# Two edits to a decoder kernel: softplus on VectorE alone with delta first, and normalisation with means and variances in turn

## The chip, the cores and the metric

The kernel runs on one core of a Trainium2 chip. Its time is device microseconds from the start to the end of one execution, and the median of several executions counts. TensorE (PE) multiplies matrices into PSUM, VectorE (DVE), ScalarE (ACT) and GpSimd (POOL) work on tiles in SBUF or PSUM, SyncE (SP) issues most DMAs. Each engine has its own in-order program, and semaphores order them against each other. All data is float32 unless said otherwise.

## The reference

A decoder of six blocks over x of shape (2, 1024, 256): a Mamba block, cross attention, a causal attention with a mixture of experts, linear attention, a second cross attention and a feed-forward net. Each block gets `_layernorm(x)` and adds its result to x. Two parts matter here.

```python
def _layernorm(x, axis=-1, eps=1e-05):
    m = jnp.mean(x, axis=axis, keepdims=True)
    v = jnp.var(x, axis=axis, keepdims=True)
    return (x - m) / jnp.sqrt(v + eps)
...
xn = _rmsnorm(x, norm_w)
...
dA = jnp.exp(d_t[..., None] * A)
dBu = (d_t * u_t)[..., None] * B_t[:, None, :]
h = dA * h + dBu
y = jnp.einsum('bdn,bn->bd', h, C_t)
```

In the Mamba block, `xn` is projected to `xm` and `z`; `xm` goes through a causal convolution of four taps and a silu and becomes u; u is projected to a low-rank part, B and C; the low-rank part is projected to delta, and delta = softplus(delta + bias). The scan over time then runs 64 states for each of 512 channels.

## The kernel before, in words

X lies channels first, 128 partitions by 2 x 2048 columns, and is worked in four chunks (`NCH`) of 512 columns (`W`).

**`norm`** (lines 91 to 215) is called nine times: for the Mamba block (start 12.71 us), its rms norm without centring and with weights (46.83), cross attention (1583.92), the decoder's outer norm (1753.25), its first norm with weights and biases (1778.86), the experts' norm with weights and biases (2341.35), linear attention (2683.59), the second cross attention (2804.14) and the feed-forward net (2880.66). TensorE forms the mean of each chunk over channels by a product with a matrix of 1/256 (L132); VectorE subtracts it (L146); ScalarE squares (L178); TensorE forms the variance the same way (L138); ScalarE takes an approximate reciprocal root (L181) and its square (L184); VectorE makes one Newton step of three operations (L152, L155, L157). Chunks 0 and 1 are scaled by GpSimd (L199), chunks 2 and 3 by VectorE (L160); with weights, ScalarE applies them last (L172). Each step runs over all four chunks before the next one begins on the same engine. The block ends with a barrier of all engines, which also waits for the weights that SyncE loads beside it.

**`scan_inputs`** (lines 420 to 719) runs once for each of two batches, starting at 67.94 and 825.90 us. TensorE makes 38 tiles in the order of a list (`order`, L446), each into one of eight PSUM banks in turn; tile n waits until tile n - 8 was taken from its bank. The 1024 columns of a batch are two halves. ScalarE takes most tiles (L551), applies silu to u (L576) and makes |delta| (L582), its exponential e (L584), max(delta, 0) (L585) and four squares of e shifted by constants (L595). log(1 + e) is then a polynomial: products of (square + constant), formed one behind the other. VectorE computes it for three of the four channel groups (`softplus_dve`, operations of 1536 columns), GpSimd for the fourth (`softplus_pool`, 12 operations of 512 columns a half). The results are delta and delta times u, which TensorE transposes (tiles `du`) and ScalarE (half 0) or VectorE (half 1) copies out. ScalarE also forms the scan's first products (L607). SyncE stores u, C and delta to DRAM and reads delta of half 0 back, spread over partitions (`near`). There is room for three squares (`ROOM`), so a fourth waits until the first was used up, by both engines.

**`scan`** follows each `scan_inputs`, with 512 scans on VectorE (L876), decays and products on ScalarE (L839, L847), weighting on GpSimd (L825) and transposes and sums on TensorE; its code is the same before and after.

## Time and profile before

| | us |
|---|---|
| median of 3 runs | 3047.18 |
| lowest, highest | 3044.08, 3047.55 |
| the profiled execution's own time | 3044.58 |
| span of its trace, first to last instruction | 3042.8 |
| mean granted TensorE clock | 0.913 of full speed |
| busy: PE, DVE | 2370.3, 1997.0 |
| busy: ACT, POOL | 1772.5, 1398.9 |

The trace is of one execution. Busy times are sums over one engine; the time between an instruction's start and the end of the idle time before it is put down to what released it. A program of this kind is a row of stages with barriers between them, so the lengths of the stages add up to the whole, and shares of busy time over the whole span say little of one stage.

### The profile page before, as it was taken

The page shows a single profiled execution, that of the slowest core. Times are in us where ns is not written, and L with a number is a line of the kernel's source. Part 1 is how long each engine was busy: PE and PEld are TensorE (multiplying, and loading weights), DVE is VectorE, ACT ScalarE, POOL GpSimd, SP SyncE. Part 2 cuts the span into 40 slices and gives each one's busy share as a digit, 9 for nine tenths or more (in the row PEclk, how much of TensorE's full clock was granted, in tenths as well). Part 3 has the DMA queues.
Part 4 walks back from the last instruction along what each step waited for, and adds up shares of the span by engine and source line. Part 5 has one row for each costly group of instructions (what it writes and reads, how often), then busy time and mean ns, then how long its engine had stood idle before and what let it go on. Part 6 is the DMA issues. An engine that isn't in the chain of part 4 may idle for free. (4 is left out here: it accounts for less than half of the span.)

```text
span 3042.8 us, 38732 instructions
## 1 busy us (share of the span) xinstructions
PE 2370.3 (78%) x12420; PEld 1202.1 (40%) x12421; DVE 1997.0 (66%) x1798; ACT 1772.5 (58%) x2733; POOL 1398.9 (46%) x540
## 2 busy tenths in 40 slices
PE   4678888888857888888886758797787499869668
PEld 1244444444324444444435123223222355545323
DVE  5689999999658999999965666515913222133440
ACT  3689999999478999999941430171064111122230
POOL 1489998999557999899941110000000300020000
PEclk7889999999988999999996878798889699979889
DMA  2130001000123000100000300010012300010000
GB/s 75 54 106 28 24 28 39 28 28 28 40 72 87 28 28 28 39 28 24 28 20 2 112 35 1 6 42 11 1 33 100 157 21 21 23 39 9 28 0 28
DMA packets 59819, 116.17 MB, mean 38 GB/s; under 512 B 13620, under 2 KB 21812, under 8 KB 58305
## 3 DMA queue, kind: packets, MB, share of 16 engines
q1 hardware_dynamic: 51104, 103.72, 10.6%
q0 software_dynamic: 8608, 11.05, 1.2%
q8 instruction: 65, 1.06, 0.1%
q14 instruction: 42, 0.34, 0.0%
HBM read 86.92 MB, written 27.53 MB: 38 GB/s over the span
## 5 line engine op out<-in xcount | busy, mean ns | idle before, releaser
L825 POOL TENSOR_TENSOR hs<-hs,c_bc 128x2048 f32<-128x2048 f32 x256 | 1166.2, 4556 | 67.0 <-DVE hs L876 49.3
L876 DVE TENSOR_TENSOR_SCAN hs<-decays,carry,ps 128x512 f32<-128x512 f32 x512 | 621.7, 1270 | 9.1 <-PE ps L903 8.4
L876 DVE TENSOR_TENSOR_SCAN hs<-decays,ps 128x512 f32<-128x512 f32 x512 | 610.9, 1215 | 21.0 <-PE ps L903 8.3
L911 PE MATMUL ps<-hs,sel 128*64 128x512 f32 x2048 | 498.4, 608 | 15.5 <-POOL hs L825 15.2
L839 ACT ACTIVATE decays<-delta_near,A 128x512 f32<-128x512 f32 x512 | 363.4, 723 | 23.2 <-DVEq L853 22.7
L903 PE MATMUL ps<-ident,dbu_even 128*128 128x128 f32 x2048 | 295.1, 283 | 91.9 <-DVE hs L876 63.2
L903 PE MATMUL ps<-ident,dbu_odd 128*128 128x128 f32 x2048 | 293.3, 282 | 92.3 <-DVE hs L876 60.6
L839 ACT ACTIVATE decays<-delta_far,A 128x512 f32<-128x512 f32 x512 | 358.8, 714 | 11.0 <-DVE hs L876 10.9
L847 ACT ACTIVATE dbu_odd<-du_turned,b_turned 128x512 f32<-128x512 f32 x512 | 360.8, 718 | 0.0
L847 ACT ACTIVATE dbu_even<-du_turned,b_turned 128x512 f32<-128x512 f32 x496 | 349.8, 718 | 0.0
L903 PEld LDWEIGHTS ps<-ident,dbu_even 128*128 128x128 f32 x2048 | 220.0, 141 | 241.9 <-DVE hs L876 192.5
L903 PEld LDWEIGHTS ps<-ident,dbu_odd 128*128 128x128 f32 x2048 | 219.6, 141 | 242.2 <-DVE hs L876 188.4
L1058 ACT ACTIVATE prob<-ps 128x1024 f32<-128x1024 f32 (+2 forms) x224 | 176.1, 837 | 161.7 <-PE ps L1029 137.5
L911 PEld LDWEIGHTS ps<-hs,sel 128*64 128x64 f32 x2048 | 124.5, 136 | 213.1 <-issue 188.0
L981 POOL DMA_DIRECT2D q<-o_rows x13 | 9.1, 698 | 399.1 <-DMA o_rows<-osb 334.4
L1183 PE MATMUL ps<-kx,qx 32*128 32x77 f32 (+4 forms) x1280 | 138.5, 553 | 53.4 <-DVE negmax L1210 30.1
L1067 DVE COPY osb<-ps 128x512 f32<-128x512 f32 x32 | 21.8, 689 | 215.5 <-PE ps L1040 215.5
L1210 DVE TENSOR_REDUCE negmax<-ps 128x4 f32<-128x2048 f32 (+4 forms) x70 | 139.0, 2029 | 23.3 <-PE ps L1188 16.6
L1614 PE MATMUL ps<-w_wv,x_turned 128*128 x304 | 141.1, 608 | 10.7 <-ACT x_turned L1673 10.7
L1709 DVE TENSOR_SCALAR hid_turned<-ps 128x512 f32<-128x512 f32 x38 | 26.3, 691 | 178.6 <-PE ps L1622 178.6
L1023 PE MATMUL ps<-qx,kx 32*128 32x512 f32 (+4 forms) x896 | 112.7, 574 | 38.7 <-PEq L1231 20.4
L199 POOL TENSOR_TENSOR XN<-XN,norm_rstd 128x1024 f32<-128x1024 f32 x8 | 18.8, 2344 | 246.5 <-DVE norm_rstd L157 246.5
(265 smaller groups left out, 2759.1 us busy)
## 6 DMA issues: line engine op xcount, KB each, us to landing
c_bc<-c_rows SPq DMA_DIRECT2D x256, 128.0 KB, 2.8
o_rows<-osb SPq DMA_DIRECT2D x32, 256.0 KB
u_rows<-u SPq DMA_DIRECT2D x4, 1024.0 KB, 8.8
d_rows<-delta SPq DMA_DIRECT2D x4, 1024.0 KB, 4.2
delta_near<-d_rows SPq DMA_DIRECT2D x4, 1024.0 KB, 9.6
hs<-u_rows SPq DMA_DIRECT2D x4, 1024.0 KB, 6.6
delta_far<-d_rows SPq DMA_DIRECT2D x4, 1024.0 KB, 12.1
w_down<-in_expert_proj SPq DMA_DIRECT2D x1, 4096.0 KB, 36.5
```

What stands on the lines that cost most here:

```text
L825: pool.tensor_tensor(x, x, spread(c_bc[:, g, :], 4), ALU.mult).then_inc(weighed.sem, 1)
L839: act.activation(decays[:, s % RING, :], (far if q else near)[:, blk, :], ACT.Exp, scale=A[:, at(i * GB, g), blk]).then_inc(decay.sem, 1)
L847: act.activation(dbu[0], dbu[1], ACT.Copy, scale=dbu[2]).then_inc(made.sem, 1)
L876: dve.tensor_tensor_scan(hs[:, quad % RING, n, :], decays[:, s % RING, :], ps[:, DBU + s % RING, :], carry[:, at(i * GB, g), blk] if q els ...
L903: mm = pe.transpose(ps[:, DBU + s % RING, t * P:(t + 1) * P], room[g % 2][:, t, blk, :, :].rearrange("p n d -> p (n d)"), k.ident[:])
L911: mm = pe.matmul(ps[lo:lo + DB, ACC + quad % 2 * 2 + j // 2, :], k.sel2[:, :], hs[:, quad % RING, j, :], start=False, stop=False, skip_gro ...
L1023: mm = pe.matmul(ps[0:krows, 2 * (m % 3) + j % 2, first:W], job.kx[rows, par, c, t * P:t * P + krows], job.qx[rows, par, c, qc * W + first ...
L1058: act.activation(prob[0:krows, m % 4, :, first:W], ps[0:krows, 2 * (m % 3):2 * (m % 3) + 2, first:W], ACT.Exp).then_inc(weighed.sem, 1)
L1183: mm = pe.matmul(ps[:, STRIPS * (f % 2) + j, at:at + m], qx[strip, par, c, t * P:(t + 1) * P], kx[strip, par, c, o:o + m], start=True, sto ...
L1210: dve.tensor_reduce(to[:, :, groups[0]:groups[0] + per], banks[:, :, :, 0:m], AX.X, ALU.max, negate=True).then_inc(maxed.sem, 1)
L1614: mm = pe.matmul(ps[:, 2 * h + g, :], xt[:, p, c, :], wv[:, bass.ds(e * (C * 2 * FF) + (c * 2 * FF + g * FF + h * HALF), HALF)], start=(c ...
L1709: dve.tensor_scalar(hid_t[:, h, :, :], ps[:, HID + h, :].rearrange("p (f n) -> p f n", f=HT), 1.0, None, ALU.mult).then_inc(hid_copied.sem, 1)
```

## The change

**In `norm`**, TensorE forms mean 0, mean 1, then a variance and a mean in turn. ScalarE squares chunk c and then takes the root of chunk c - 1, and begins with a root of one column that has no use but that it is the first of its kind. The Newton step is written with a third, small operation on ScalarE (the root times -0.5) and two on VectorE instead of three: (v r r - 3)(-r / 2). VectorE centres chunk c ahead of inverting chunk c - 2.

```diff
+            def means(c):
...
+            for c in range(NCH + 1):
+                if centre and c < NCH:
+                    means(c)
+                if c:
+                    variances(c - 1)
+
...
-                dve.tensor_scalar(rstd[:, c, :], rstd[:, c, :], -0.5, 1.5, ALU.mult, ALU.add).then_inc(corrected.sem, 1)
-                dve.wait_ge(corrected.sem, corrected.at(c + 1))
-                dve.tensor_tensor(rstd[:, c, :], rstd[:, c, :], r0[:, c, :], ALU.mult).then_inc(rstd_ready.sem, 1)
-                if c >= BY_POOL:
-                    dve.wait_ge(rstd_ready.sem, rstd_ready.at(c + 1))
-                    dve.tensor_tensor(chunk(dst, c), chunk(body, c), spread(rstd[:, c, :], C),
-                                      ALU.mult).then_inc(scaled_dve.sem, 1)
+                dve.wait_ge(halved.sem, halved.at(c + 1))
+                dve.scalar_tensor_tensor(rstd[:, c, :], rstd[:, c, :], 3.0, r0[:, c, :], ALU.subtract, ALU.mult)\
+                   .then_inc(rstd_ready.sem, 1)
...
+            for c in range(NCH + 2):
+                if centre and c < NCH:
+                    centre_chunk(c)
+                if c >= 2:
+                    invert(c - 2)
+                    if c - 2 >= BY_POOL:
+                        scale(c - 2)
...
+            def root(c):
+                act.wait_ge(var_ready.sem, var_ready.at(c + 1))
+                act.activation(r0[:, c, :], ps[:, VAR + c, :], ACT.Abs_reciprocal_sqrt,
+                               bias=k.eps[:, 0:1] if eps == EPS else k.eps[:, 1:2]).then_inc(root_ready.sem, 1)
+                act.wait_ge(root_ready.sem, root_ready.at(c + 2))
+                act.activation(r0sq[:, c, :], r0[:, c, :], ACT.Square).then_inc(root_squared.sem, 1)
+                act.wait_ge(root_squared.sem, root_squared.at(c + 1))
+                act.activation(r0[:, c, :], r0[:, c, :], ACT.Copy, scale=-0.5).then_inc(halved.sem, 1)
+
...
+            act.activation(first[:], k.eps[:, 0:1], ACT.Abs_reciprocal_sqrt).then_inc(root_ready.sem, 1)
+            for c in range(NCH + 1):
+                if c < NCH:
+                    square(c)
+                if c:
+                    root(c - 1)
```

**In `scan_inputs`**, all of the polynomial is VectorE's, in operations of 2048 columns. The list of tiles has delta right behind the low-rank part, and `z` of half 1 last. ScalarE takes |x| and max(x, 0) straight from the PSUM bank, by Abs and Relu with the bias, and e lies in the room of `du_turned` instead of `xm`. SyncE stores u of both halves first.

```diff
-    e_ = xm[:, :, :].rearrange("p c n -> p (c n)")[:, 0:CPB * CI * W].rearrange("p (h c n) -> p h c n", h=CPB, c=CI)
+    e_ = du_t[:, :, :].rearrange("p (h c) n -> p h c n", h=CPB)
...
-                                                 ("C", 0, 1), ("delta", 0, CI), ("B", 0, 1), ("z", 1, CI),
-                                                 ("low", 1, 1), ("C", 1, 1), ("delta", 1, CI), ("B", 1, 1),
-                                                 ("du", 0, QT), ("du", 1, QT)) for m in range(tiles)]
+                                                 ("delta", 0, CI), ("C", 0, 1), ("low", 1, 1),
+                                                 ("delta", 1, CI), ("C", 1, 1), ("B", 0, 1), ("B", 1, 1),
+                                                 ("z", 1, CI), ("du", 0, QT), ("du", 1, QT)) for m in range(tiles)]
...
-            def take_delta(h):
+            def magnitude_of(h):
                 for m in range(CI):
-                    take("delta", h, m, delta[:, m, h * W:(h + 1) * W], ACT.Identity, bias=vec[:, m, DC + 1:DC + 2])
+                    act.wait_ge(summed.sem, summed.at(index["delta", h, m] + 1))
+                    act.activation(e_[:, h, m, :], bank(("delta", h, m)), ACT.Abs, bias=vec[:, m, DC + 1:DC + 2])\
+                       .then_inc(magnitude.sem, 1)
+
+            def positive_of(h):
+                for m in range(CI):
+                    take("delta", h, m, delta[:, m, h * W:(h + 1) * W], ACT.Relu, bias=vec[:, m, DC + 1:DC + 2])
...
             silu_u(0)
             take_z(0)
             take_low(0)
-            take_delta(0)
+            magnitude_of(0)
+            silu_u(1)
+            exponential(0)
+            squares(0, range(ROOM))
+            positive_of(0)
+            take_low(1)
+            magnitude_of(1)
+            squares(0, range(ROOM, PAIRS))
+            exponential(1)
+            positive_of(1)
             take_b(0)
-            silu_u(1)
+            take_b(1)
+            squares(1, range(PAIRS))
             take_z(1)
-            exponential(0)
-            squares(0)
-            take_low(1)
-            take_delta(1)
-            take_b(1)
-            exponential(1)
-            squares(1)
             first_products()
...
-            for h in range(CPB):
-                softplus_pool(pool, h)
...
+
+            store_u(0)
+            sp.wait_ge(u_stored.sem, u_stored.at(16))
+            store_u(1)
+            store_c(0)
+            sp.wait_ge(c_stored.sem, c_stored.at(16))
+            store_delta(0)
+            sp.wait_ge(d_stored.sem, d_stored.at(16))
+            spread_delta(k, sp, b, 0, near, d_near)
+            store_c(1)
+            store_delta(1)
```

`softplus` is `softplus_dve` with `part` and `DVE_PART` gone, and without the wait for `positive`; `softplus_pool` is gone.

What stands on ScalarE in the normalisation at 1583.92, before and then now (`norm_r` is the root, `norm_r0sq` its square):

```order
L178 ACTIVATE norm_sq<-XN 128x1024 x4
L181 ACT_TABLE_LOAD
L181 ACTIVATE norm_r_67<-ps,eps 128x512
L184 ACTIVATE norm_r0sq<-norm_r_67 128x512
L181 ACTIVATE norm_r_67<-ps,eps 128x512
L184 ACTIVATE norm_r0sq<-norm_r_67 128x512
```

```order
L205 ACT_TABLE_LOAD
L205 ACTIVATE norm_first<-eps 128x1
L184 ACTIVATE norm_sq<-XN 128x1024 x2
L188 ACTIVATE norm_r_69<-ps,eps 128x512
L191 ACTIVATE norm_r0sq<-norm_r_69 128x512
L193 ACTIVATE norm_r_69<-norm_r_69 128x512
L184 ACTIVATE norm_sq<-XN 128x1024
L188 ACTIVATE norm_r_69<-ps,eps 128x512
```

The table load stands at the front, and the first root comes behind two squares instead of four.

On VectorE in a norm (the first call, whose chunks lie in `dbu_even`), before and then now:

```order
L146 TENSOR_TENSOR dbu_even<-X,ps 128x2x512 x4
L152 SCALAR_TENSOR_TENSOR norm_rstd<-ps,norm_r0sq 128x512
L155 TENSOR_SCALAR norm_rstd<-norm_rstd 128x512
L157 TENSOR_TENSOR norm_rstd<-norm_rstd,norm_r_21 128x512
L152 SCALAR_TENSOR_TENSOR norm_rstd<-ps,norm_r0sq 128x512
```

```order
L152 TENSOR_TENSOR dbu_even<-X,ps 128x2x512 x3
L159 SCALAR_TENSOR_TENSOR norm_rstd<-ps,norm_r0sq 128x512
L163 SCALAR_TENSOR_TENSOR norm_rstd<-norm_rstd,norm_r_21 128x512
L152 TENSOR_TENSOR dbu_even<-X,ps 128x2x512
L159 SCALAR_TENSOR_TENSOR norm_rstd<-ps,norm_r0sq 128x512
```

The fourth centring stands behind the inversion of chunk 0.

On ScalarE in `scan_inputs` of the first batch, from the take of half 0's low-rank part (`low`) on, before and then now. `xm` and, now, `du_turned` hold e:

```order
L551 ACTIVATE low<-ps 128x512
L551 ACTIVATE delta<-ps,mamba_vec 128x512 x4
L551 ACTIVATE b_turned<-ps 128x256
L576 ACTIVATE u<-u,mamba_vec 128x512 x4
L551 ACTIVATE zs<-ps 128x512 x4
L582 ACTIVATE xm<-delta 128x2048
L584 ACT_TABLE_LOAD
L584 ACTIVATE xm<-xm 128x2048
L585 ACTIVATE delta<-delta 128x4x512
L595 ACTIVATE sp_square<-xm,roots 128x2048 x4
L551 ACTIVATE low<-ps 128x512
```

```order
L572 ACTIVATE du_turned<-ps,mamba_vec 128x512 x4
L583 ACTIVATE u<-u,mamba_vec 128x512 x4
L588 ACT_TABLE_LOAD
L588 ACTIVATE du_turned<-du_turned 128x2048
L597 ACTIVATE sp_square<-du_turned,roots 128x2048 x3
L552 ACTIVATE delta<-ps,mamba_vec 128x512 x4
L552 ACTIVATE low<-ps 128x512
L572 ACTIVATE du_turned<-ps,mamba_vec 128x512 x4
L597 ACTIVATE sp_square<-du_turned,roots 128x2048
L588 ACTIVATE du_turned<-du_turned 128x2048
```

`z` of half 1 (`zs`) no longer stands ahead of the exponential, the fourth square stands behind the Abs of half 1, and later in the same program `zs` has a table load of its own, as has the first decay of `scan`.

## Rows read from the trace of the kernel before

**Rows 1.** Busy time by stretch: bounds, length, busy us (instructions) per engine, clock, DMA.
```profile
12.71:40.40 27.69, 16.38 (x32) 6.91 (x32) 17.59 (x18) 11.69 (x14) 4.69 (x2) 0.83 0.24 86
46.83:67.63 20.80, 8.99 (x16) 3.70 (x16) 12.71 (x14) 14.38 (x20) 4.69 (x2) 0.75 0.00 0
1583.92:1609.18 25.26, 13.97 (x32) 5.96 (x32) 17.58 (x18) 10.45 (x13) 4.68 (x2) 0.85 0.15 48
...
1778.86:1805.95 27.09, 15.66 (x32) 6.61 (x32) 17.60 (x18) 15.24 (x20) 4.69 (x2) 0.81 0.25 97
2341.35:2368.18 26.83, 13.97 (x32) 5.96 (x32) 17.59 (x18) 16.52 (x21) 4.68 (x2) 0.83 0.95 370
2683.59:2710.46 26.87, 15.56 (x32) 6.61 (x32) 17.60 (x18) 10.45 (x13) 4.69 (x2) 0.82 0.13 42
2804.14:2828.00 23.86, 13.97 (x32) 5.97 (x32) 17.59 (x18) 9.27 (x12) 4.69 (x2) 0.90 0.11 28
...
67.94:166.50 98.56, 61.45 (x152) 29.01 (x152) 56.97 (x53) 58.65 (x66) 46.94 (x29) 0.78 0.26 77
825.90:922.55 96.65, 58.37 (x152) 27.93 (x152) 55.89 (x53) 56.99 (x64) 43.96 (x24) 0.81 0.23 68
166.80:806.00 639.20, 537.67 (x3088) 285.18 (x3088) 618.53 (x516) 623.41 (x1016) 594.07 (x192) 0.99 0.12 38
```

**Rows 2.** Timeline of the normalisation at 1583.92: start, us, engine, line, operation [idle before].
```profile
1585.91 1.22 DVE L146 TENSOR_TENSOR XN<-X,ps 128x1024 f32<-128x1024 f32 x1 [2.31 <-PE ps L132]
...
1587.16 1.06 ACT L178 ACTIVATE norm_sq<-XN 128x1024 f32<-128x1024 f32 x1 [34.65 <-DVE XN L146]
...
1593.39 1.28 ACT L181 ACT_TABLE_LOAD   x1
...
1594.68 0.69 ACT L181 ACTIVATE norm_r<-ps,eps 128x512 f32<-128x512 f32 x1
...
1595.40 0.63 ACT L184 ACTIVATE norm_r0sq<-norm_r 128x512 f32<-128x512 f32 x1
...
1596.14 0.69 DVE L152 SCALAR_TENSOR_TENSOR norm_rstd<-ps,norm_r0sq 128x512 f32<-128x512 f32 x1 [3.86 <-ACT norm_r0sq L184]
...
1598.10 2.35 POOL L199 TENSOR_TENSOR XN<-XN,norm_rstd 128x1024 f32<-128x1024 f32 x1 [37.08 <-DVE norm_rstd L157]
...
1598.65 2.07 DVE L155 TENSOR_SCALAR norm_rstd<-norm_rstd 128x512 f32<-128x512 f32 x1
```

**Rows 3.** Timeline of the first batch's scan inputs, by engine.
```profile
94.36 0.60 ACT L551 ACTIVATE low<-ps 128x512 f32<-128x512 f32 x1 [2.83 <-PE ps L542]
...
102.42 2.55 ACT L576 ACTIVATE u<-u,mamba_vec 128x512 f32<-128x512 f32 x4
...
116.19 5.77 ACT L595 ACTIVATE sp_square<-xm,roots 128x2048 f32<-128x2048 f32 x3
...
97.83 3.70 PE L526 MATMUL ps<-low,dbu_odd 128*128 128x512 f32 x8
...
125.90 5.81 PE L526 MATMUL ps<-low,dbu_odd 128*128 128x512 f32 x8 [10.05 <-ACT low L551]
...
118.21 1.76 DVE L473 SCALAR_TENSOR_TENSOR sp_poly<-sp_square,xm 128x1536 f32<-128x1536 f32 x1 [19.59 <-ACT sp_square L595]
120.11 4.68 DVE L473 SCALAR_TENSOR_TENSOR sp_poly<-sp_square,sp_poly 128x1536 f32<-128x1536 f32 x2
...
127.09 2.70 DVE L475 SCALAR_TENSOR_TENSOR sp_poly<-xm,sp_poly 128x1536 f32<-128x1536 f32 x1
...
168.50 2.33 DVE L876 TENSOR_TENSOR_SCAN hs<-decays,ps 128x512 f32<-128x512 f32 x2 [2.00 <-PE ps L903]
...
120.53 2.64 POOL L501 TENSOR_TENSOR sp_poly<-sp_poly,sp_square 128x512 f32<-128x512 f32 x1
...
160.72 1.26 POOL L505 TENSOR_TENSOR u<-delta,u 128x512 f32<-128x512 f32 x1
```

**Rows 4.** Groups of VectorE by shape: count | busy us, mean ns | idle before.
```profile
L1930 DVE TENSOR_TENSOR tern_room<-tern_room,w 128x2048 f32<-128x2048 f32 x2 | 4.6, 2292 | 0.1
```

More of the change, by code:

```diff
@@ L207, in norm @@
         centred.passed(NCH)
[L208 removed]
+    for s in (squared, var_ready, root_squared, newton, halved, rstd_ready):
         s.passed(NCH)
+    root_ready.passed(NCH + 1)
     scaled.passed(BY_POOL)
@@ new lines, in softplus @@
+                dve.wait_ge(soft.sem, soft.at(n + f))
+            dve.scalar_tensor_tensor(poly[:], square[:, (h * PAIRS + f) % ROOM], b, poly[:] if f else e,
+                                     ALU.add, ALU.mult).then_inc(soft.sem, 1)
+        dve.wait_ge(soft.sem, soft.at(n + PAIRS))
+        dve.scalar_tensor_tensor(poly[:], e, LOG1P_REAL, poly[:], ALU.add, ALU.mult).then_inc(soft.sem, 1)
+        dve.wait_ge(soft.sem, soft.at(n + PAIRS + 1))
+        dve.wait_ge(taken.sem, taken.at(take_no["delta", h, CI - 1]))
@@ L578, in exponential, with squares @@
             def exponential(h):
-                x = delta[:, :, h * W:(h + 1) * W]
-                act.wait_ge(taken.sem, taken.at(take_no["delta", h, CI - 1]))
-                act.activation(e_[:, h], x, ACT.Abs).then_inc(magnitude.sem, 1)
-                act.wait_ge(magnitude.sem, magnitude.at(h + 1))
+                act.wait_ge(magnitude.sem, magnitude.at((h + 1) * CI))
                 act.activation(e_[:, h], e_[:, h], ACT.Exp, scale=-1.0).then_inc(e_ready.sem, 1)
-                act.activation(x, x, ACT.Relu).then_inc(positive.sem, 1)
                 act.wait_ge(e_ready.sem, e_ready.at(h + 1))
-            def squares(h):
-                for f in range(PAIRS):
+            def squares(h, which):
+                for f in which:
                     n = h * PAIRS + f
@@ L678, in _, with store_u @@
             d_rows = k.d_rows[b].rearrange("(c p) t -> p c t", p=P)
-            for h in range(CPB):
+            def store_u(h):
                 cols = slice(h * W, (h + 1) * W)
```

121 lines of the change are left out of this document (41 added, 80 removed).

## The prediction

> **What bounds the kernel now.** I read first how long each stage lasts, then the timeline inside one normalisation, then the timeline of the scan inputs. [rows 1] gives a length per stage. The column after the bounds is the length, then come the busy times. The nine calls of `norm` last 20.8 to 27.7 us each, and in none is an engine busy for the whole length: VectorE has 12.7 to 17.6, TensorE 9.0 to 16.4, ScalarE 9.3 to 16.5, GpSimd 4.7. A stage in which nobody is full is bound by a chain. `scan_inputs` lasts 98.56 and 96.65 us for the two batches, with VectorE at 57, ScalarE at 59 and GpSimd at 47: a chain again. `scan` (639.2 us a batch) has ScalarE at 623 and VectorE at 619, and its code is not changed.
>
> [rows 2] is the normalisation that starts at 1583.92. VectorE centres a chunk 1.99 us after the start (four matmul passes of 0.43 us and 0.28 us until VectorE moves). ScalarE squares it (1.06), but the first root comes only at 1594.68: all means stand ahead of the variances on TensorE, all squares ahead of the roots on ScalarE, and a table load of 1.28 us lies between. Then each chunk takes root 0.69, square 0.63, three operations on VectorE. While GpSimd scales a chunk (2.35 us), the multiply-add of L155 lasts 2.07 us instead of 0.43, the time in which GpSimd works. Operations with one input in PSUM (L152, 0.69) are not held up.
>
> [rows 3] is the first batch. `low` of half 0 is taken at 94.36, but ScalarE reaches the exponential only after `z` of half 1, and VectorE stands idle 19.59 us before its first product at 118.21. Two neighbouring products of 1536 columns take 4.68 us, one alone 1.76, while a GpSimd product that starts at 120.53 takes 2.64: the two engines hold each other up. The last product is GpSimd's at 160.72; the stage ends at 166.50.
>
> **The change, part by part.**
>
> *Normalisation, centred, without weights.* I chain the new order with the same durations, from 0: mean 0 to 1.71; centred 1.99 to 3.21; squared 3.24 to 4.30; variance 0 from 4.35 to 6.06 (TensorE waits 0.9 us behind mean 1, all that the new wait costs); then mean 2 to 7.78, variance 1 to 9.49, mean 3 to 11.21. VectorE centres chunk 3 from 11.49 to 12.71. Queued behind it are the two operations on chunk 1 (0.69 each), which end at 14.03. GpSimd scales chunk 1 until 16.40. The second operation on chunk 2 has both inputs in SBUF and is late next: it ends 0.55 after GpSimd, at 16.95. Then scale 2 (1.22), two operations (0.69 each) and scale 3 (1.22), with 0.03 us between dependent ones and 0.08 us of overlap between others, give 20.78. The same chain for the old order gives 24.95, and the trace has 25.26, so the new one should last 21.1: **4.2 us less**. The early activation costs nothing, its load lies in the 1.99 us in which ScalarE has nothing to square. The extra ScalarE operation (0.63) ends at 12.25 for chunk 1 and delays nobody.
>
> This holds for four calls (1583.92 and two like it, at 1753.25 and 2880.66, and 2683.59, where the slow clock adds the same to both orders): 16.8 us. The first call (27.69) has the clock down for some 5 us, through all means; in the new order only the first means meet it before the chain turns to other engines: 5.0. The one at 2804.14 had no load inside (23.86): 2.8. Of the two with weights and biases, ScalarE becomes the end: its last halving comes at 17.8, then eight operations of 0.76 us ((16.52 - 10.45) / 8), 23.9 against 26.83: 2.9 at 2341.35, and 2.0 at 1778.86, which had no load to lose. The uncentred one (20.80) gains 0.7: its squares now queue behind roots. Sum **30.2 us** over nine calls.
>
> *Scan inputs.* Up to the take of `low` at 94.36 to 94.96 nothing moves. `delta` (0.86 us a tile, from 3.70 for four with the drain) now starts at once instead of behind C, at 95.0. The four Abs straight from PSUM end at 99.4, silu of half 1 (2.55) at 101.9, table load 103.2, Exp (taken as a square of the same form, 1.93) 105.1, three squares 110.8. The four Relu (0.61 each) and `low` of half 1 end at 113.7. `delta` of half 1 then finds the clock down, as at 125.90 (5.81 us where 3.70 is the full-speed price), since TensorE has idled 8 us: the Abs end at 119.6, the fourth square of half 0 at 121.6. That is the new wait: VectorE has finished its third product at 113.9 and stands still for 7.8 us. From there VectorE is never idle: four operations of half 0 to 131.0, C 0.6, seven of half 1 to 147.9, and the last transposes and copies (now from 160.72 + 1.26 to 166.50: 4.5) 152.4, against 166.50: **14.1 us less a batch**. The operations of 2048 columns are new; none in this stage shows them. L1930 takes 2.29 with both inputs in SBUF [rows 4], four thirds of 1.76 are 2.35, and four thirds of the longest, 2.70 at 127.09 [rows 3], are 3.6. I take 2.30, the nearest row in form, since with GpSimd gone nothing is left to contend. Both batches: 28.2 us.
>
> The removed GpSimd work (24 operations) was on the path and takes nothing with it. Stores: u of half 1 now leaves at 102, so its multiply does not wait; delta of half 1 leaves at 145.6 and has 7 us to land before the stage ends.
>
> *Table loads.* Silu of `z` 1 now comes after the exponentials, so each batch gets one more load there, in ScalarE's slack (it would be idle 7 us at the end), and one more at the first decay of `scan`. VectorE's first scan waits 2.00 us for TensorE at 168.50 [rows 3]; a decay 1.28 us later is 0.4 us too late at least, 1.28 at most because ScalarE is 97% busy there. I take 0.9 each, **1.8 us back**. The trace has 1.28 us for a load and the next activation starts 0.01 us after it (1593.39, 1594.68). The Trainium skill (ScalarE: Activation LUTs, What ACT_TABLE_LOAD costs) adds about 1.38 us of draining, 2.66 us in all; by that the scan starts would cost up to 2.8 us more, and the forecast 2993. The trace does not agree: nothing of that kind lies between the last square and the root.
>
> **Sum.** 30.2 + 28.2 - 1.8 = 56.6 us off the profiled execution's 3044.58: 2988.0. The median of the runs is 2.6 us above that execution, so I forecast **2990**.
>
> **The rivals.**
> *The clock (slower than before).* Now TensorE runs means and variances in one unbroken stretch; the new order has breaks of 0.9 us between chunks. If the granted clock fell to 1.2 GHz for them, four passes would take 3.41 instead of 1.71 us, and the same chain ends at 31.6 without weights and 35.3 with them, that is 3.9 to 7.7 us worse than now for the six and 8.2 and 8.5 for the two, 52 us in all, against 27 won elsewhere: 3044.6 + 25 + 2.6 = 3072. It decides where a centred call gets more than 3.4 us (27 / 8) longer than now. Against it: in `scan` TensorE is busy 538 of 639 us with many short breaks and keeps 0.99 [rows 1]; the new norm has it busy 14.0 of 15.6 us. The Trainium skill (TensorE: Matmul & The Clock Gate, Part 1) speaks for the danger in kind: idleness throttles the array again. 3%.
> *The wide operations are slow by themselves.* If 2.70 us were the price of such an operation and not contention, 2048 columns would take 3.6, fourteen of them 50 us after 107, and the stage would end where it does now: 3044.6 - 30.2 + 1.8 + 2.6 = 3019. For: 4.68 for two. Against: 1.76 for the same operation when GpSimd does not read. 5%.
> *Norms give half.* If ScalarE's three operations a chunk or GpSimd's hold of VectorE cost more than I chain, or the affine tail grows: 15 us less, 3005. 10%.
> *More comes.* After each norm TensorE idles some 12 us now, with the clock down at the next stage; idling 5.6 us less, it may keep it, up to 2.0 us (8.99 for the sixteen passes of the call at 46.83, 13.97 / 2 at full speed) at five places: 2980. 12%.
> *It doesn't do what it says*: the order of instructions shows the new order on each engine, so only a wait can undo it. Under 1%.
>
> **How the numbers follow.** The forecast itself has 69%. Its own bounds are 2.29 to 2.35 us for the wide operations (2 us over both batches), 0.8 to 2.6 for the scan starts, and 1 us per norm: 2980 to 3002. The range 2976 to 3008 adds the cases of half-norms and more clock, and leaves out the other two and their neighbourhood. About 0.2% (6 us) is what a measurement can tell from no change. Faster 0.95; within 0.2% 0.02; slower 0.03, the clock.
>
> **What would show it.** Right: norms without weights last 21.1 us, with GpSimd's second scaling starting 14 us in; the wide operations last 2.3 us each; VectorE idles about 8 us after three of them in half 0 and hardly after; `scan_inputs` lasts 84.5 us; nine norms lose 30 us together. Wrong: a granted clock under 0.8 while a norm's matmuls run, wide operations over 2.6 us, DMA or ScalarE ahead of the last copy of the stage, or a `scan` longer by more than 3 us.

## The result, and the profile after

The changed kernel takes **2993.19 us** (median of 4 runs, 2991.77 to 2994.59), against 3045.63 for the kernel before (4 runs, 3042.93 to 3047.55): ratio 0.9831, 95% interval [0.9816, 0.9847]. The span of the profiled execution is 2990.6 us, 52.2 shorter than that of before.

| | before | after |
|---|---|---|
| nine calls of `norm`, sum of their lengths, us | 229.3 | 197.6 |
| scan inputs, batch 0 and 1, us | 98.56, 96.65 | 85.17, 83.07 |
| from the start of `scan` to the next stage, batch 0 and 1, us | 659.1, 661.1 | 664.8, 660.4 |
| span, us | 3042.8 | 2990.6 |

A norm's length runs from its first matmul to its last operation (the uncentred one from its first operation of ScalarE, the decoder's outer norm up to the start of the norm behind it); that of the scan inputs from the first matmul to VectorE's last copy. The norms give 31.7 us, the inputs 27.0, and `scan` with the projection behind it takes 5.0 back. That makes 53.7; the span fell by 52.2, so the rest of the program took 1.5 more.

By stage, as [rows 1] shows it of before (stretch, its length, then busy time and instructions of PE, PEld, DVE, ACT and POOL, the granted clock, DMA share, GB/s; the stretch of the second batch's scan inputs, 812.05 to 895.39, runs on to the start of `scan`, 0.27 us behind the last copy):

```profile
12.62:35.31 22.69, 16.74 (x32) 6.65 (x32) 13.04 (x14) 13.16 (x18) 4.71 (x2) 0.98 0.29 105
41.85:61.85 20.00, 10.09 (x16) 3.76 (x17) 8.34 (x10) 16.38 (x26) 4.72 (x2) 0.76 0.00 0
61.85:147.02 85.17, 60.21 (x152) 27.34 (x152) 57.42 (x53) 57.13 (x71) 3.17 (x5) 0.82 0.29 90
...
812.05:895.39 83.34, 58.10 (x152) 26.41 (x152) 57.41 (x53) 55.47 (x69) 0.00 (x0) 0.88 0.27 79
1555.82:1576.72 20.90, 14.50 (x32) 5.80 (x32) 13.05 (x14) 13.24 (x18) 4.71 (x2) 1.00 0.19 59
1744.68:1769.73 25.05, 15.99 (x32) 6.45 (x32) 13.06 (x14) 17.61 (x25) 4.72 (x2) 0.84 0.27 105
```

The norm at 1555.82 is the one of [rows 2]. It lasts 20.90 us instead of 25.27, with the clock granted in full. Its timeline (start, length, engine, line, operation, then in brackets the idle time before and who ended it):

```profile
1562.20 0.69 ACT L188 ACTIVATE norm_r<-ps,eps 128x512 f32<-128x512 f32 x1 [0.36 <-PE ps L139]
...
1565.05 0.68 DVE L159 SCALAR_TENSOR_TENSOR norm_rstd<-ps,norm_r0sq 128x512 f32<-128x512 f32 x1
...
1569.97 2.35 POOL L225 TENSOR_TENSOR XN<-XN,norm_rstd 128x1024 f32<-128x1024 f32 x1 [1.08 <-DVE norm_rstd L163]
...
1571.72 1.15 DVE L163 SCALAR_TENSOR_TENSOR norm_rstd<-norm_rstd,norm_r 128x512 f32<-128x512 f32 x1
...
1575.49 1.23 DVE L168 TENSOR_TENSOR XN<-XN,norm_rstd 128x1024 f32<-128x1024 f32 x1
```

The first root stands 6.4 us behind the start, where it was 10.8. GpSimd's second scaling starts 14.15 us in. The operation at 1571.72 has both inputs in SBUF and ends 0.55 us after GpSimd (1572.32), as the chain had it.

The scan inputs of batch 0, VectorE and ScalarE from the exponential on, beside [rows 3]:

```profile
96.57 1.91 ACT L588 ACTIVATE du_turned<-du_turned 128x2048 f32<-128x2048 f32 x1
...
98.52 5.79 ACT L597 ACTIVATE sp_square<-du_turned,roots 128x2048 f32<-128x2048 f32 x3
100.55 2.29 DVE L498 SCALAR_TENSOR_TENSOR sp_poly<-sp_square,du_turned 128x2048 f32<-128x2048 f32 x1 [4.16 <-ACT sp_square L597]
102.95 4.69 DVE L498 SCALAR_TENSOR_TENSOR sp_poly<-sp_square,sp_poly 128x2048 f32<-128x2048 f32 x2
...
107.23 6.38 PE L528 MATMUL ps<-low,dbu_odd 128*128 128x512 f32 x8 [7.93 <-ACT low L552]
...
116.26 2.29 DVE L498 SCALAR_TENSOR_TENSOR sp_poly<-sp_square,sp_poly 128x2048 f32<-128x2048 f32 x1 [8.62 <-ACT sp_square L597]
...
126.05 2.27 DVE L498 SCALAR_TENSOR_TENSOR sp_poly<-sp_square,du_turned 128x2048 f32<-128x2048 f32 x1
...
140.20 2.29 DVE L507 TENSOR_TENSOR u<-delta,u 128x2048 f32<-128x2048 f32 x1
```

Each operation of 2048 columns takes 2.29 us. VectorE starts its first 38.7 us into the stage (50.3 before), then stands still 8.62 us for the fourth square, because ScalarE waits in between for `delta` of half 1, which runs at the low clock (6.38 us). In batch 1 the wait is 8.05 us. From 116.26 VectorE is never idle up to its last product.

What took back 5.0 us is in `scan`, whose code is unchanged. At its start in batch 0, and at the eight `skip` matmuls (L906, four times in the program):

```profile
147.37 1.28 ACT L852 ACT_TABLE_LOAD   x1 [6.81 <-PEq L509]
...
149.48 1.22 DVE L889 TENSOR_TENSOR_SCAN hs<-decays,ps 128x512 f32<-128x512 f32 x1 [2.46 <-ACT decays L852]
...
161.47 4.81 PE L906 MATMUL ps<-hs,diag_skip 128*128 128x512 f32 x8
...
478.84 6.62 PE L906 MATMUL ps<-hs,diag_skip 128*128 128x512 f32 x8 [2.50 <-DMA hs<-u_rows]
...
909.58 4.51 PE L906 MATMUL ps<-hs,diag_skip 128*128 128x512 f32 x8
...
1226.57 3.70 PE L906 MATMUL ps<-hs,diag_skip 128*128 128x512 f32 x8 [2.42 <-DMA hs<-u_rows]
```

Before the change the same eight matmuls took these times, in the order batch 0 half 0, half 1, batch 1 half 0, half 1:

```profile
178.58 3.60 PE L893 MATMUL ps<-hs,diag_skip 128*128 128x512 f32 x8
...
495.29 5.40 PE L893 MATMUL ps<-hs,diag_skip 128*128 128x512 f32 x8 [2.61 <-DMA hs<-u_rows]
...
935.74 3.61 PE L893 MATMUL ps<-hs,diag_skip 128*128 128x512 f32 x8
...
1251.93 5.40 PE L893 MATMUL ps<-hs,diag_skip 128*128 128x512 f32 x8 [2.52 <-DMA hs<-u_rows]
```

The eight are two passes for each of four tiles; at 2.4 GHz they take 3.6 to 3.7 us, and the longer they ran at 1.2 GHz the longer the sum, 6.6 at the most. VectorE's twelfth scan is followed by a wait for them: the granted clock of 147 to 153 us is 1.00, that of the next 12 us 0.55 and 0.59. Two theories stand for the 5.0 us. One is the table load at the first decay, fixed by the new order. The other is where TensorE's clock happens to fall, which would differ from one execution to the next.

### The profile page after: what moved, and what is told of

The parts are those of the page before. It is cut to its first block and busy times, and to the rows that moved or that the text cites. A ratio compares the mean times of both kernels' runs of the same rounds, so it can differ in the third digit from the quotient of the medians.

```text
span 2990.6 us, 38704 instructions
## 1 busy us (share of the span) xinstructions
PE 2374.3 (79%) x12420; PEld 1200.4 (40%) x12421; DVE 1957.9 (65%) x1762; ACT 1794.5 (60%) x2789; POOL 1311.3 (44%) x492
## 5 line engine op out<-in xcount | busy, mean ns | idle before, releaser
L852 ACT ACTIVATE decays<-delta_near,A 128x512 f32<-128x512 f32 x512 | 356.4, 707 | 3.2 <-DVE hs L889 3.2
L1036 PE MATMUL ps<-qx,kx 32*128 32x512 f32 (+4 forms) x896 | 112.4, 572 | 38.7 <-PEq L1244 20.4
L1384 POOL DMA_INDIRECT rows<-ys,slot x16 | 15.2, 949 | 249.3 <-ACTq L1380 244.7
```

The lines of the kernel that those rows point to most:

```text
L852: act.activation(decays[:, s % RING, :], (far if q else near)[:, blk, :], ACT.Exp, scale=A[:, at(i * GB, g), blk]).then_inc(decay.sem, 1)
L1036: mm = pe.matmul(ps[0:krows, 2 * (m % 3) + j % 2, first:W], job.kx[rows, par, c, t * P:t * P + krows], job.qx[rows, par, c, qc * W + first ...
```

## The experiments

Each kernel ran beside the kernel before on the same chip, so the ratios compare; before had 3044.04 beside the first four kernels, 3044.36 beside the second four, 3050.54 beside the last four. "Stage" below is the length of the scan inputs in batch 0 and 1, from the first matmul to the start of `scan`: 98.8 and 96.9 before, 85.4 and 83.3 in the changed kernel.

**The changed kernel again.** No edit.

> The changed kernel once more, as the yardstick of the three kernels beside it. Its profile tells whether the 5.6 us by which the first batch's scan and projection grew (664.76 us from the start of scan to the next stage, against 659.13 before) are a property of the new order or chance of one execution. If they come from the table load at the first decay and from the place at which TensorE's clock falls, both of which are fixed by the order, they appear again within 1 us, and the eight matmuls of `skip` take 4.8 and 6.6 us in batch 0 and 3.7 us in the second half of batch 1, as in the first profile. If they are chance, the two batches show other numbers, with differences of 2 us or more between the two executions. Time: 2993 us, within 0.1%.

Measured: 2992.43 us, ratio 0.9833 [0.9819, 0.9846]. The norms (197.9) and the inputs (85.7, 83.6) repeat. The four `skip` groups take 4.39, 3.70, 4.68 and 6.59 us: the half that was slow has changed from half 1 of batch 0 to half 1 of batch 1.

```profile
1222.53 6.59 PE L906 MATMUL ps<-hs,diag_skip 128*128 128x512 f32 x8 [2.45 <-DMA hs<-u_rows]
```

From its first scan to the end of its last, `scan` takes 635.1 and 631.8 us in the first profile and 631.5 and 634.9 here. So 3 us of a batch's `scan` are chance. What repeats is the first stretch: 32 scans take 41.6 and 41.4 us, then 41.2 and 41.5, where before had 38.9 and 40.1.

**The Exp load taken early.**

```diff
+            def exp_again():
+                act.activation(next_exp[:], k.eps[:, 0:1], ACT.Exp)
...
             take_z(1)
+            exp_again()
             first_products()
```

> The changed kernel with one more activation (Exp of one column) in the scan inputs behind the last `z`, where ScalarE otherwise waits 7 us for the last product. The table load moves there. If the load is what delays the start of scan, the first decay starts at the start of the block, VectorE's first scan waits 2.0 us as before the change instead of 2.5, and each batch starts 0.4 to 1.3 us earlier: 1 to 2.6 us less in all, 2991. Rival: what scan lost comes from TensorE's clock at `skip` and not from the load; then the start moves but the end of the first 32 scans (41.6 us, against 38.9 before the change, in batch 0) stays over 40.5 us, and the time is 2993. Since the new start moves the phase of the clock, the eight `skip` matmuls can also take another of the three lengths seen, 3.6, 5.4 or 6.6 us.

Measured: 2987.06 us, ratio 0.9810 [0.9797, 0.9823].

```profile
134.53 1.28 ACT L614 ACT_TABLE_LOAD   x1
...
148.15 0.72 ACT L857 ACTIVATE decays<-delta_near,A 128x512 f32<-128x512 f32 x1 [5.30 <-DVEq L871]
...
149.79 1.22 DVE L894 TENSOR_TENSOR_SCAN hs<-decays,ps 128x512 f32<-128x512 f32 x1 [2.00 <-PE ps L921]
```

The first scan waits 2.00 us for TensorE as in [rows 3], and the first 32 take 39.6 and 40.0 us. The load at the decay costs 0.46 us at the first scan of batch 0 and 0.93 at that of batch 1. By the twelfth scan it has cost its whole length: from the start of `scan` to that scan 14.94 us pass in both batches before the change and here, and 16.21 to 16.22 in the changed kernel, 1.28 more. Behind the twelfth scan VectorE waits for `skip` and the turns behind it: from its start to the next scan's 5.0 to 5.4 us pass in the changed kernel and 4.1 to 4.2 here. Together that makes 2.1 to 2.5 us a batch, some 4.6 in all. The median gained 5.4 us where I expected 1 to 2.6; the intervals allow either.

**Keeping TensorE's clock at `skip`.**

```diff
+                if q:
+                    pe.wait_ge(gated.sem, gated.at((q - 1) * CI + 1))
+                    warm(14)
                 pe.wait_ge(u_here.sem, u_here.at(16 * (q + 1)))
...
+                    if first and q == 0 and quad == 2:
+                        warm(10)
                     for s in range(4 * quad, 4 * quad + 4):
                         turn(q, i, s)
+                        if first and q == 0 and quad < 2:
+                            warm(3)
```

(`warm(n)` is n transposes of the identity into the first accumulator bank.)

> The changed kernel with transposes of the identity into an accumulator bank that is free, on TensorE in the stretches where it waits ahead of the eight `skip` matmuls (three behind each of the first eight turns, ten ahead of the ninth, and 14 while `u` of the second half is in flight). If the difference between the batches (5.6 us longer against 0.7 shorter) is TensorE's clock at this place, the granted clock stays at 1.00 there, the eight matmuls take 3.4 to 3.7 us at all four places instead of 4.8, 6.6 and 3.7, and VectorE's waits behind the 12th and the 268th scan fall from 5.4 and 6.6 us to about 3: 1 to 3 us less at three of four places, 4 to 8 us in all, 2985 to 2989. Rival: the waits are those for the `u` rows in flight and for the queue behind them; then TensorE's extra work only delays it, and the time is 2993 to 2996.

Measured: 2991.85 us, ratio 0.9830 [0.9816, 0.9843]. The four groups take 3.60, 3.70, 3.60 and 3.70 us:

```profile
157.23 1.58 PE L903 MATMUL ps<-ident 128*128 128x128 f32 x13
...
161.05 3.60 PE L913 MATMUL ps<-hs,diag_skip 128*128 128x512 f32 x8
...
477.51 3.70 PE L913 MATMUL ps<-hs,diag_skip 128*128 128x512 f32 x8 [0.69 <-DMA hs<-u_rows]
```

From the start of the twelfth scan to the next now 3.1 us pass in both batches, from the 268th 3.5 and 3.6, and the two scans last 630.1 and 630.2 us, 6.1 less together than in the repetition. So the clock is what lengthened `skip`. It also parts the cost of the table load. That load is still here, and the twelfth scan starts 16.22 us into `scan` as in the changed kernel, but the wait behind it is as short as the best of the kernel before (3.06). So the load's own price is 1.28 us a batch, and the other 1 us that the early load won behind the twelfth scan was TensorE's clock at `skip` and in the turns around it. How much that is differs from run to run: in the kernels without the transposes the wait is 3.9 to 5.5 us with the load and 3.0 to 4.2 without. Yet span and median gained only 2.0 and 0.6 us, where I expected 4 to 8: between the scans 114.2 us passed instead of 112.0, and behind them 1463.4 instead of 1461.9. At the end of the first scan four sums and the first projection matmuls met the low clock this time (16.86 us for 32 passes instead of 15.67). That it was the edit that moved the low clock there is not shown: in the first profile of the changed kernel, without the edit, the last groups of sums met it too (3.13 and 3.29 us for eight passes, 1.94 in the repetition).

**The squares ahead of `delta` of half 1.**

```diff
-            squares(0, range(ROOM))
+            squares(0, range(1))
+            take_low(1)
             positive_of(0)
-            take_low(1)
+            squares(0, range(1, PAIRS))
             magnitude_of(1)
-            squares(0, range(ROOM, PAIRS))
```

> The changed kernel with ScalarE's order in the scan inputs altered: one square of half 0, then `low` of half 1, the positive parts of half 0, the other three squares, the magnitudes of half 1. This takes away the 8.6 us that VectorE waits for the fourth square in each batch. If VectorE's chain is what ends the stage from its first product on, as the prediction says, only some 2.3 us of that wait is left, in one piece ahead of the second product, and the stage gets 5 to 7 us shorter a batch: 10 to 14 us less, 2979 to 2983. Rival: ScalarE or the stores end the stage (the last ScalarE copies come only 3 us before the end); then the wait moves to the second half's first square or to the last copies, and less than 4 us are won in all, 2989 or more.

Measured: 2978.60 us, ratio 0.9783 [0.9770, 0.9797]; the stages last 80.7 and 77.7 us, 4.8 and 5.7 less.

```profile
106.75 7.08 DVE L498 SCALAR_TENSOR_TENSOR sp_poly<-sp_square,sp_poly 128x2048 f32<-128x2048 f32 x3 [2.39 <-ACT sp_square L597]
```

The wait is 2.39 us, and from 106.75 VectorE is not idle again until its last product. So VectorE's chain does end the stage. The runs gained 13.8 us on the repetition, 3.4 more than the two stages; in the profiles the two `scan`s are 2.7 shorter together than in the repetition, chance as above.

**The new `norm` alone**, in the kernel before.

> The kernel before with the new `norm` alone. The normalisations are separate stages, so their gain should be there without the scan inputs': 30 us less, 3015, with 24 to 34 as bounds. Rival: part of it is a loan from the clock, since the stage behind each norm begins at another phase of TensorE's clock in this kernel than in the changed one; then the whole differs from 30 us by more than 5. A norm between two projections should last 20.9 us here as in the changed kernel.

Measured: 3013.38 us, ratio 0.9897 [0.9878, 0.9917], 31 us less. The norms sum to 198.2. Against the 2992.4 us of the changed kernel's repetition that leaves 21 us for the edit of the scan inputs.

**The order of `norm` undone**, the other two parts kept.

```diff
-            for c in range(NCH + 1):
-                if centre and c < NCH:
-                    means(c)
-                if c:
-                    variances(c - 1)
+            if centre:
+                for c in range(NCH):
+                    means(c)
+            for c in range(NCH):
+                variances(c)
```

(VectorE's and ScalarE's loops likewise.)

> The changed kernel with the old order in `norm` (all means ahead of all variances on TensorE, all centrings, all squares), but with the early activation and the two operations on each chunk kept. My chain of durations, which gave 20.8 us for a centred norm in the new order and 24.95 in the old kernel's, gives 21.8 for this one: the order by itself is worth 1.0 us a call, 8 to 10 us in all with the first call at the low clock, 3001. Rival: the order is what brings most of the 4.2 us (TensorE's turn was the visible wait); then it costs 3 us a call or more, 24 us in all, and the time is 3015 or more.

Measured: 2997.64 us (2995.45 to 3005.56), ratio 0.9844 [0.9828, 0.9861]. The call between the projections lasts 22.01 us (20.90 in the changed kernel), the first 25.00 (22.69), all nine 206.2 (197.6): 8.6 us, as expected; the median rose by 5, the profiled execution was the slowest of the four. The uncentred norm is shorter in the old order, 19.1 us against 19.8. The root comes later and the chunks crowd into GpSimd's time:

```profile
1574.85 1.77 DVE L163 SCALAR_TENSOR_TENSOR norm_rstd<-norm_rstd,norm_r 128x512 f32<-128x512 f32 x1
...
1576.70 2.35 POOL L224 TENSOR_TENSOR XN<-XN,norm_rstd 128x1024 f32<-128x1024 f32 x1 [0.63 <-DVE norm_rstd L163]
...
1577.26 2.34 DVE L163 SCALAR_TENSOR_TENSOR norm_rstd<-norm_rstd,norm_r 128x512 f32<-128x512 f32 x1
```

**The early activation left out.**

```diff
-            act.activation(first[:], k.eps[:, 0:1], ACT.Abs_reciprocal_sqrt).then_inc(root_ready.sem, 1)
```

> The changed kernel without the early activation in `norm`, so that the table load stands ahead of the first root again. In the old order it was on the path (1.28 us, the chain gives 1.3). In the new order ScalarE has 0.9 us and more to spare at that place, since VectorE comes to the first chunk's inversion only behind its third centring, and the chain gives the same 20.8 us: no change, 2993, within 2 us. Rival: the load delays the second or third square and with it TensorE's variances; then up to 1.28 us at each of seven calls, 9 us, 3002.

Measured: 2992.53 us, ratio 0.9832 [0.9816, 0.9848]; norms 197.7. In the new order the load is covered:

```profile
1562.03 1.28 ACT L188 ACT_TABLE_LOAD   x1
...
1565.22 0.68 DVE L159 SCALAR_TENSOR_TENSOR norm_rstd<-ps,norm_r0sq 128x512 f32<-128x512 f32 x1
```

VectorE's inversion starts 9.2 us behind the norm's start with and without it, behind its third centring.

**Three operations a chunk again, no halving.**

```diff
+                dve.tensor_scalar(rstd[:, c, :], rstd[:, c, :], -0.5, 1.5, ALU.mult, ALU.add).then_inc(halved.sem, 1)
                 dve.wait_ge(halved.sem, halved.at(c + 1))
-                dve.scalar_tensor_tensor(rstd[:, c, :], rstd[:, c, :], 3.0, r0[:, c, :], ALU.subtract, ALU.mult)\
-                   .then_inc(rstd_ready.sem, 1)
+                dve.tensor_tensor(rstd[:, c, :], rstd[:, c, :], r0[:, c, :], ALU.mult).then_inc(rstd_ready.sem, 1)
...
-                act.wait_ge(root_squared.sem, root_squared.at(c + 1))
-                act.activation(r0[:, c, :], r0[:, c, :], ACT.Copy, scale=-0.5).then_inc(halved.sem, 1)
```

> The changed kernel with the old three operations of VectorE on each chunk and no halving on ScalarE. The chain gives 22.2 us against 20.8 for a centred norm, since the multiply-add of 0.43 us has both ends in SBUF and waits while GpSimd works: 1.4 us for each of the six centred calls without weights, and in the three with weights ScalarE's missing 0.63 us a chunk gives back up to 2.5 us that the end waits for. In all 5 to 9 us more, 3000. Rival: VectorE has slack enough between the chunks (13.0 of 20.9 us busy) and the third operation costs nothing: 2993, or less because of ScalarE.

Measured: 2999.34 us, ratio 0.9857 [0.9840, 0.9873]. The call between the projections lasts 22.29 us, all nine 207.3, 9.7 more. The small multiply-add meets GpSimd at work and lasts 1.35 us instead of 0.43:

```profile
1574.44 1.35 DVE L162 TENSOR_SCALAR norm_rstd<-norm_rstd 128x512 f32<-128x512 f32 x1
```

**VectorE alone, in the old order.** The order of tiles as it was before, and on ScalarE:

```diff
             magnitude_of(0)
+            positive_of(0)
+            take_b(0)
             silu_u(1)
+            take_z(1)
             exponential(0)
-            squares(0, range(ROOM))
-            positive_of(0)
+            squares(0, range(PAIRS))
             take_low(1)
             magnitude_of(1)
...
```

The Abs and Relu straight from the bank stay as in the changed kernel.

> The changed kernel with the old order of tiles and of ScalarE's work in the scan inputs, and the logarithm on VectorE alone. It parts the two halves of that change. VectorE's first product then comes at about 116 us of the first batch as before, seven operations of 2.29 us last 16.0 us against 24.7 (118.21 to 142.9 in the old kernel), and the second half starts when ScalarE has its first square, at about 138: the stage ends at about 160 instead of 166.5, so 6 to 7 us of the 13.5 a batch come from VectorE alone and 6 to 8 from the order. Time 2993 + 13 to 15 = 3007. Rival: the order alone is the gain, because ScalarE's arrival sets both halves; then 3015 or more.

Measured: 2996.89 us, ratio 0.9829 [0.9812, 0.9845], where I expected 3007. The stages last 87.2 and 85.6 us: what is kept here, VectorE alone with the Abs and Relu from the bank, is worth 11.6 and 11.3, the order 1.8 and 2.3.

```profile
108.21 2.29 DVE L498 SCALAR_TENSOR_TENSOR sp_poly<-sp_square,du_turned 128x2048 f32<-128x2048 f32 x1 [16.14 <-ACT sp_square L597]
...
127.93 2.29 DVE L498 SCALAR_TENSOR_TENSOR sp_poly<-sp_square,du_turned 128x2048 f32<-128x2048 f32 x1 [2.66 <-ACT sp_square L597]
```

Here the first product comes 46.3 us into the stage, 7.6 later than in the changed kernel and 4.0 earlier than before, mainly because the two wide operations for |x| and max(x, 0), 1.90 and 1.89 us, are gone from ScalarE's way; the four Relu in their place (2.42 us) fill the time in which ScalarE waited for `z` of half 1 before. My expectation had left that out. It also misread the old kernel: its 24.7 us run on into half 1, to 142.9. VectorE's seven operations of half 0 end at 134.62, 16.4 us behind their start, and GpSimd's last one at 139.15:

```profile
131.91 2.71 DVE L481 TENSOR_TENSOR u<-delta,u 128x1536 f32<-128x1536 f32 x1
...
137.88 1.27 POOL L505 TENSOR_TENSOR u<-delta,u 128x512 f32<-128x512 f32 x1
```

So VectorE needs 16.5 us for all four channel groups alone (108.21 to 124.67) and needed 16.4 for three beside GpSimd, while GpSimd's fourth group took 24.6 (114.57 to 139.15). From its first product VectorE waits 2.66 us in all, where the changed kernel waits 8.62: the order wins 7.6 us and gives 6.0 back. No load lies at the start of `scan` either, and the first 32 scans take 38.9 us in both batches, 2.7 and 2.4 less: so with the old order the whole is the same within what this measurement can tell.

**GpSimd at work beside VectorE.**

```diff
+            x = xm[:, 0:2, 0:T]
...
+            for n in range(6):
+                pool.tensor_tensor(x, x, x, ALU.subtract).then_inc(beside.sem, 1)
```

> The changed kernel with six operations of GpSimd on 2048 columns beside the logarithm, on `xm`, which nobody reads any more. Nothing of the result changes. If GpSimd at work on SBUF holds VectorE's operations with both inputs there, each waits until GpSimd's operation is over: they last up to 4.5 us more, 6 such holds a batch less the 8.6 us of idle time, so 14 to 20 us more a batch and 3021 to 3033. Rival: they share the bandwidth, as the 2.70 us against 1.76 of the old kernel could also say (1.5 times); then the seven of half 0 last 3.5 us each, most of that goes into the idle 8.6 us, and the time is 2993 to 3000.

Measured: 3012.43 us, ratio 0.9878 [0.9861, 0.9894], about 14 us more by the ratio; the stages last 95.5 and 93.0, 19.8 more together or 10 a batch, where I expected 14 to 20 a batch. The profiled execution is 7 us shorter than the median of the four, and its scans are 3.0 us shorter than in the first profile.

```profile
99.70 31.63 POOL L678 TENSOR_TENSOR xm<-xm 128x2048 f32<-128x2048 f32 x6 [34.61 <-ACT du_turned L589]
...
105.56 16.70 DVE L499 SCALAR_TENSOR_TENSOR sp_poly<-sp_square,sp_poly 128x2048 f32<-128x2048 f32 x3
...
122.30 5.57 DVE L502 SCALAR_TENSOR_TENSOR sp_poly<-du_turned,sp_poly 128x2048 f32<-128x2048 f32 x1
...
133.51 2.29 DVE L508 TENSOR_TENSOR u<-delta,u 128x2048 f32<-128x2048 f32 x1
```

An operation of 2.29 us lasts 5.57 beside GpSimd and 2.29 again once GpSimd is done. GpSimd's own line shows the other side (minimum, median and maximum in ns of its twelve operations):

```profile
L678 POOL TENSOR_TENSOR xm<-xm x12: 3598/5527/5529, 99.7 to 878.5; 128x2048 f32<-128x2048 f32 x12
```

The shortest, 3.60 us, is the first of each batch, which starts 2 us ahead of VectorE's first product; the others take 5.53. So the two engines take turns. Their operations become equally long, 5.57 and 5.53 us, though alone they need 2.29 and at most 3.60. GpSimd's last ends at 131.33 (99.70 + 31.63), 3.46 us behind the end of VectorE's last but one (127.87); VectorE's last beside it ends at 133.48, 2.15 us behind that. One round is 5.6 us, and each engine gets its work done from the other's end on. It is the hold, then, and not shared bandwidth; my price for it came from GpSimd's operation of this width in `scan` (4.56 us), where this one needs 3.60 at the most. The Trainium skill (SBUF — State Buffer, Who interferes with whom) calls the port pair of the two an exclusive lock, and this trace agrees. Six holds lose 18 us (the first 1.5), VectorE's 8.6 us of idle time take up part, and the stage grows by 10.

**TensorE at work behind the variances.**

```diff
+            if centre:
+                pe.wait_ge(centred.sem, centred.at(NCH))
+            for n in range(20):
+                pe.matmul(ps[:, 0, :], k.inv[:, :], sq[:, n % NCH, 0, :], start=True, stop=True)
```

> The changed kernel with 20 more matmuls of 512 columns on TensorE behind the last variance of each norm, into a bank that nobody reads, so that it works until the norm ends. It asks whether the clock lost behind a norm can be had back, my fourth rival. If so, the first eight matmuls of the projection behind the cross norm take 3.5 us instead of 6.41, and 2 to 3 us are won at each of six to nine places: 2970 to 2980. Rival: the clock falls in the 1.6 us between the norm and the next stage all the same, or these matmuls are not on the path: 2993, or some us more where the added matmuls run at the low clock and outlast the norm.

Measured: 3081.81 us, ratio 1.0102 [1.0086, 1.0119]. I had counted a matmul of 512 columns as one pass; it is two, so the twenty last 17.2 us and outlast the norm, which grows to 33.05 us, all nine by 101.0. But the first eight passes of the projection behind it now run at 2.4 GHz:

```profile
1611.29 3.67 PE L294 MATMUL ps<-XN,wq 128*128 128x512 f32 x8 [1.58 <-PEq L349]
```

against, in the changed kernel, with the granted clock of that stretch at 0.54:

```profile
1578.32 6.41 PE L290 MATMUL ps<-XN,wq 128*128 128x512 f32 x8 [6.63 <-PEq L345]
```

The span grew by 90.6 us and not by 101.0, so some 10 us came back at nine places, of which 3 us or so may be chance, and 2.7 at this one. With half as many matmuls that might be a gain; it was not tried.

**The three edits of the scan and its inputs together**: the early load, the transposes and the new order of squares, the latter with `low` of half 1 released ahead of the positive parts.

> The changed kernel with the three edits of the scan and its inputs together: the early Exp load (2987.1 alone), the work for TensorE's clock at `skip` (2991.9) and the new order of the squares (2978.6). If they are independent, 2978.6 - 5.4 - 0.6 = 2972.6. The order differs in one point from the run before: `low` of half 1 is released to TensorE ahead of the positive parts, so its matmuls start 2.4 us earlier, which VectorE's wait hides. Rival: the early load takes the slack of ScalarE at the end of the stage, which the new order has used up (it was idle there for 7 us, now for less): then the load's gain is lost, 2978.

Measured: 2976.20 us beside 3050.54, ratio **0.9759 [0.9743, 0.9776]**, the lowest of all. Scaled to the other runs' 3044 us that is 2971 us, near the 2972.6 expected, and so it beats both kernels. The stages last 80.5 and 77.4 us, the scans 630.3 and 630.8. The twelfth scan starts 14.97 us into `scan` and the next one 3.05 behind it: with both edits neither the load nor the clock costs anything there. The load does find room:

```profile
125.32 1.28 ACT L555 ACT_TABLE_LOAD   x1
...
128.70 1.28 ACT L616 ACT_TABLE_LOAD   x1
...
132.01 5.02 ACT L612 ACTIVATE dbu_even<-du_turned,b_turned 128x512 f32<-128x512 f32 x8
```

ScalarE's last product ends at 137.03; VectorE's last copies begin at 138.70.

## Why the prediction was right

It said 2990 us, and 2993 was measured. The sum was 2988.0 for the profiled execution, which took 2993.08, 5.1 more. The 2.6 us added for the distance between median and profiled execution brought the forecast nearer, but that distance was 0.1 us after the change and 1.05 before it (3045.63 less 3044.58): that part was luck. Step by step:

- **Norms, 30.2 us less: right.** The lengths fell by 31.7. The calls that I chained to 21.1 us last 20.90 to 20.92 between projections, the first fell by 5.00 (5.0), the one without a load by 2.94 (2.8), the two with weights and biases by 2.0 and 3.3 (2.0 and 2.9), the uncentred one by 1.0 (0.7). The chain also stood when it was taken apart: the order 1.1 us a call (1.0 expected), the two-operation step 1.4 (1.4), the early load nothing. Undone one at a time they are 2.5 of the 4.4 us that such a call gained: each covers some of another's cost. The prediction gave the early activation no price of its own; in this order it has no use. In the order of before the same load cost 1.42 us: 25.28 with it, 23.86 at the call that had none.
- **Wide operations at 2.30 us: right**, 2.29. The rival that they are slow by themselves is refuted, and the kernel with GpSimd beside them shows what the 2.70 us of [rows 3] was.
- **14.1 us a batch from the scan inputs: right in size**, 13.4 and 13.6. The wait that I expected for the fourth square, 7.8 us, was 8.62; 0.6 of that is the low clock, which lasted through all of `delta` of half 1 (6.38 us against 5.81 before). In batch 1 it was 8.05. What the sum did not tell is which part earns it: it ran through both at once. With the old order 11.5 are left (4.0 of them ahead of the first product, mainly by ScalarE's shorter way), and the order adds 2, which the longer start of `scan` that comes with it takes back (2.7 and 2.4). The Abs and Relu from the bank were not tried apart from VectorE alone.
- **Scan starts, 1.8 us back: too small**, 5.0 were measured. The loads themselves are 2.6 of them, 1.28 a batch, the upper bound that I gave: ScalarE, busy 97%, makes up for none of it by the twelfth scan. The step that failed is that the sum held nothing for TensorE's clock at `skip`. The wait behind the twelfth scan grew from 3.06 and 4.18 us to 5.37 and 5.07, and with the clock kept it is 3.05, with the load or without. The rest runs the other way (the wait behind the 268th scan grew by 1.1 us in batch 0 and fell by 1.8 in batch 1) and is within the 3 us by which each `scan` differs between two executions of the same kernel. I had named a `scan` longer by more than 3 us as a sign of error, and in batch 0 it was one: 5.6 us, 1.3 of them the load and 2.3 the wait behind the twelfth scan.
- **The clock rival: refuted.** With breaks of up to 0.7 us ahead of a variance the granted clock of the norm at 1555.82 is 1.00, and in the one at 1744.68 it is 0.84 where it was 0.81. That more comes behind the norms did not happen: TensorE idles 6.63 us there instead of 12.90, but the next stage's first eight passes take 6.41 us where they took 5.76, and the clock there is 0.54. The Trainium skill (TensorE: Matmul & The Clock Gate, Part 1) says that idleness throttles the array again; the trace agrees for the 6.63 us behind a norm, while these short breaks left the clock at 1.00.

## What to carry to other kernels

When an order is changed so that an engine starts earlier, follow the same engine to its end: of 7.6 us won ahead of the first product 6.0 were lost again to one square that stood behind a slow `delta`, and moving that square was worth more than the whole reordering. Sharing elementwise work in SBUF between VectorE and GpSimd can cost more than it saves: here VectorE does four channel groups alone in 16.5 us, where three beside GpSimd took it 16.4 and GpSimd's fourth took 24.6. A table load moved into an engine that is busy to 97% costs its whole length, though the first wait shows only a part of it (0.46 and 0.93 of 1.28 us); an activation of one column in slack takes it away. And what a delay costs by TensorE's clock further on is a term of its own.

## What was not expected of the hardware

An operation of VectorE with two inputs in SBUF went from 2.29 to 5.57 us while GpSimd worked, and GpSimd's from 3.60 to 5.53: they take turns, whole operation by whole operation. The eight matmuls of `skip`, the same at every place, took from 3.6 to 6.6 us by where the clock fell, and two executions of one kernel differed in which batch had the 6.6. With some transposes ahead of them they took 3.6 and 3.7 at all four places.
